# Seven of sixteen gate-weighted expert sums moved from VectorE to ScalarE and GpSimd

## The reference, cut to what matters

```
h      = swiglu(flat @ W1_shared)                  # 512 hidden numbers a row
routed = 0
for e in range(8):
    routed = routed + h @ W2_experts[e] * w[:, e:e + 1]   # w: the gate of row and expert
out = x + (shared + routed)
y   = rmsnorm(out) ; x = x + layernorm(y)
```

## Time and profile before

| what | value |
|---|---|
| median of three runs | 2315.79 us |
| the profiled execution, its own time | 2326.53 us |
| its span | 2324.5 us |
| TensorE busy | 2059.2 us (89%) |
| VectorE busy | 1385.1 us (60%) |
| ScalarE busy | 831.0 us (36%) |
| GpSimd busy | 342.1 us (15%) |
| mean clock granted to TensorE | 0.881 of full speed |

### The profile page before, as it was taken

One profiled execution on the slowest core, in us unless ns is written; L12 is line 12 of the kernel. 1 busy time (PEld: TensorE's weight loads), 2 busy tenths in 40 slices (PEclk: granted clock), 3 DMA queues, 4 the chain that ended last, 5 costly groups with the idle time before them and its releaser, 6 DMA issues.

```text
span 2324.5 us, 31756 instructions
## 1 busy us (share of the span) xinstructions
PE 2059.2 (89%) x9200; PEld 1081.4 (47%) x9200; DVE 1385.1 (60%) x4293; ACT 831.0 (36%) x1714; POOL 342.1 (15%) x647
## 2 busy tenths in 40 slices
PE   6868799898999989999898988989889999999986
PEld 4343445535364443635445353453635445354445
DVE  6456455755757465674667556476575745747454
ACT  2423424262433424334242532326233252423410
POOL 3322113101320003100031011210112001210000
PEclk7566889998998987989899898799899897889998
DMA  4003002010030101201021000211002110020212
GB/s 165 2 28 136 1 2 92 37 38 10 9 130 1 48 1 66 72 2 48 1 83 56 31 17 1 83 55 38 11 2 100 37 48 1 7 90 34 74 55 91
DMA packets 23089, 104.69 MB, mean 45 GB/s; under 512 B 3312, under 2 KB 14192, under 8 KB 18288
## 3 DMA queue, kind: packets, MB, share of 16 engines
q1 hardware_dynamic: 21168, 89.81, 10.7%
q0 software_dynamic: 1728, 12.58, 1.4%
HBM read 84.56 MB, written 16.78 MB: 44 GB/s over the span
## 4 chain that ended last, share of the span: by engine, by line
PE 68%; DVE 20%; issue 7%; ACT 3%; DMA 1%; DVEq 0%; POOL 0%; SPq 0%; POOLq 0%; ACTq 0%
PE fb L734 13%; PE fb L712 11%; PE sm L646 10%; PE ot L686 10%; PE st L672 5%; PE st L615 3%; DVE negmax L1013 2%; DVE acc L1201 2%; DVE stats L927 2%; PE st L631 2%; PE dn L615 2%; PE dn L654 2%; PE dn L698 2%; PE sm L672 2%; DVE sm L1010 1%
## 5 line engine op out<-in xcount | busy, mean ns | idle before, releaser
L536 ACT ACTIVATE probs<-st 128x512 f32<-128x512 f32 (+3 forms) x832 | 404.7, 506 | 486.1 <-PE st L672 438.6
L646 PE MATMUL sm<-k_t,q_t 48*128 48x512 f32 (+3 forms) x928 | 385.8, 496 | 102.6 <-DVE negmax L1010 49.3
L734 PE MATMUL fb<-w_r,h_r 128*128 128x512 f32 x1536 | 444.9, 426 | 13.2 <-DVE acc L1201 13.2
L1013 DVE TENSOR_REDUCE negmax<-sm 128x1 f32<-128x512 f32 x464 | 302.1, 686 | 136.2 <-PE sm L646 135.5
L646 PEld LDWEIGHTS sm<-k_t,q_t 48*128 48x128 f32 x928 | 170.8, 213 | 439.4 <-DVE negmax L1010 211.3
L672 PE MATMUL st<-q_t,k_t 64*128 64x512 f32 (+3 forms) x832 | 352.2, 478 | 14.3 <-ACT probs L536 12.1
L734 PEld LDWEIGHTS fb<-w_r,h_r 128*128 128x128 f32 x1536 | 279.8, 195 | 126.4 <-issue 60.1
L712 PE MATMUL fb<-xn_t,wup_s 128*128 128x512 f32 x512 | 321.5, 723 | 6.5 <-DVE h_s L1186 4.1
L1010 DVE CUSTOM_DVE_ANT_0 sm<-sm,mask_qk 128x384 f32<-128x384 f32 (+2 forms) x464 | 213.3, 467 | 190.9 <-PE sm L646 188.5
L686 PE MATMUL ot<-probs,v_s 128*32 128x512 f32 (+3 forms) x2048 | 276.3, 563 | 2.9 <-POOL probs L439 1.8
L672 PEld LDWEIGHTS st<-q_t,k_t 64*128 64x128 f32 x832 | 153.2, 203 | 135.1 <-ACT probs L536 87.1
(11 more groups left out here) (166 smaller groups left out, 2464.1 us busy)
## 6 DMA issues: line engine op xcount, KB each, us to landing
w_r<-w_parts SPq DMA_DIRECT2D x32, 2048.0 KB, 7.8
w_parts<-w_r POOLq DMA_DIRECT2D x4, 2048.0 KB, 8.9
x_s<-in_L_attn_query SPq DMA_DIRECT2D x8, 512.0 KB, 4.6
h_s<-in_L_ffn_W_experts POOLq DMA_DIRECT2D x8, 512.0 KB, 6.3
q_t<-rot_b SPq DMA_DIRECT2D x256, 4.0 KB
x_kept<-o_s SPq DMA_DIRECT2D x8, 512.0 KB, 3.0
xa<-x_kept SPq DMA_DIRECT2D x8, 512.0 KB, 3.5
out<-acc SPq DMA_DIRECT2D x8, 512.0 KB, 11.4
```

Source lines behind the costliest of these rows:

```text
L536: nc.scalar.activation(probs[:, n % PSLOTS, 0:hi - lo], score_bank(m)[:, 0:hi - lo], ACT.Exp, scale=float(D) ** -0.5).then_inc(s_ex, 1)
L646: mm(max_bank(w)[:, 0:hi - lo], q_t[r:r + MROW, b, t * P:(t + 1) * P], k_t[r:r + MROW, b, lo:hi], start=True, stop=True).then_inc(s_sm, 1)
L734: last = mm(fb[q % 2][:, :], h_r[:, h, m, rows], w2_r[:, k % 2, w, m, :], start=(m == 0 and n == 0), stop=(m == NH - 1 and n == 2))
L1013: return v.tensor_reduce(negmax[:, g % 2, n // GH, c:c + 1], max_bank(g * UNITS + n)[:, 0:hi - lo], AX.X, ALU.max, negate=True).then_inc(s ...
```

## The change

Seven sets leave VectorE's list: 4, 5 and 6 (the middle) and 9 to 12 (the lead of attention 1). For these ScalarE multiplies both halves of the PSUM bank by their gates into `scaled[q % 2]`, which is a view of `sg`, and signals the bank as read; GpSimd adds the two halves to `acc`, one after the other. In the middle ScalarE does its three sets between the centring and the copy of the transposed rows; in the lead it does each one step behind the set's last matmuls. GpSimd does sets 4 to 6 ahead of the low parts of the second heads stage, and 9 to 12 behind them. VectorE waits for the adds (s_ad) before its own next set. A further small step tells ScalarE that the gates are ready. The last batch does the same seven sets the same way.

```
+SCALED_MID, SCALED_LEAD = (4, 5, 6), (9, 10, 11, 12)
+SCALED = SCALED_MID + SCALED_LEAD
+        scaled = [sg[:, p, :].rearrange("p (e n) -> p e n", e=2) for p in range(2)]
...
 (gpsimd)
+            def add_scaled(f, outs):
+                for q in outs:
+                    t, n = (q - NT) % NT, SCALED.index(q)
+                    pool.wait_ge(s_er, f * N_ER + q + 1)
+                    g.tensor_tensor(acc[:, t, :], acc[:, t, :], scaled[q % 2][:, 0, :], ALU.add).then_inc(s_ah, 1)
+                    pool.wait_ge(s_ah, f * N_AH + n + 1)
+                    g.tensor_tensor(acc[:, t, :], acc[:, t, :], scaled[q % 2][:, 1, :], ALU.add).then_inc(s_ad, 1)
...
                 mask_probs(i, i - 1)
+                add_scaled(i - 1, SCALED_MID)
                 low_parts(i, 1)
+                add_scaled(i - 1, SCALED_LEAD)
             for n in range(NH):
                 hidden_low(B - 1, n)
+            add_scaled(B - 1, SCALED)
...
 (scalar)
+                    if f is not None and a == 1:
+                        for q in SCALED_LEAD:
+                            if OUT_AT[NH * OUT_BESIDE.index(q) + NH - 1] + ACT_LAG == m:
+                                scale_out(f, q)
...
+            def scale_out(f, q):
+                k, t = divmod(q - NT, NT)
+                n = SCALED.index(q)
+                act.wait_ge(s_eo, f * N_EO + q + 1)
+                act.wait_ge(s_er, f * N_ER + q)
+                if n == 0:
+                    act.wait_ge(s_gate, f + 1)
+                same = [m for m in range(n) if SCALED[m] % 2 == q % 2]
+                if same:
+                    act.wait_ge(s_ad, f * N_AD + same[-1] + 1)
+                for half in range(2):
+                    last = nc.scalar.activation(scaled[q % 2][:, half, :], fb[q % 2][:, half * E:(half + 1) * E], ACT.Copy,
+                                                scale=gate[:, t, 2 * k + half:2 * k + half + 1])
+                last.then_inc(s_er, 1)
...
                 centre(i)
+                if f is not None:
+                    for q in SCALED_MID:
+                        scale_out(f, q)
                 copy_rows(i, 2)
...
 (vector)
-                signal(v.tensor_tensor(gate[:, :, 0:EPG], ew[:, :, :], gate[:, :, EPG:NE], ALU.subtract))
+                done(v.tensor_tensor(gate[:, :, 0:EPG], ew[:, :, :], gate[:, :, EPG:NE], ALU.subtract))
+                v.memset(spare[:, :], 0.0).then_inc(s_gate, 1)
...
             def expert_out(f, q):
+                if q in SCALED:
+                    return
...
                 dve.wait_ge(s_er, f * N_ER + q)
+                dve.wait_ge(s_ad, f * N_AD + sum(n < q for n in SCALED))
...
             def finish(f):
                 dve.wait_ge(s_er, (f + 1) * N_ER)
+                dve.wait_ge(s_ad, (f + 1) * N_AD)
```

More of the change, by code:

```diff
@@ L223, in build @@
         s_er, N_ER = sem("expert_out_read"), OUTS
+        s_ah, N_AH = sem("first_scaled_part_added"), len(SCALED)
+        s_ad, N_AD = sem("scaled_parts_added"), len(SCALED)
+        s_gate = sem("gates_ready")
         s_xk, s_xb = sem("x1_stored"), sem("x1_loaded_back")
@@ L544, in attention @@
                             gate_exp(f, GATE_EXPS_AT.index(m))
+                    if f is not None and a == 1:
+                        for q in SCALED_LEAD:
+                            if OUT_AT[NH * OUT_BESIDE.index(q) + NH - 1] + ACT_LAG == m:
+                                scale_out(f, q)
+                    if f is not None and a == 0:
                         for n in range(2 * NH):
@@ L599, in _ @@
             hidden_high(B - 1, 2 * NH - 1)
+            for q in SCALED:
+                scale_out(B - 1, q)
         @block.tensor
@@ L1195, in expert_out @@
                     return
-                if q == NT:
+                if q == min(q for q in range(NT, OUTS) if q not in SCALED):
                     settle()
```

## The result

The changed kernel took 2342.95 us (17 runs, 2324.67 to 2374.09) against 2313.97 for the kernel before on the same chips: a ratio of 1.0111, with a 95% interval of 1.0081 to 1.0142. It is slower; the forecast was 2294 and the range ended at 2320. Medians here are of all runs; the ratios compare fast runs alone, those within 1.5% of their kernel's fastest. What happened begins as rival C has it (one long wait before the transposes, a fall of the clock behind it), and most of the loss stands in the lead, where C had none.

A forecast was written before the change was run, and what follows sets the result against it. TensorE was taken as the bound, with most VectorE adds standing behind it. Lead -12.9, middle +3.5 and clock -12 gave -21.4 us on 2326.53, so 2305.1; less 10.7 for that execution lying above the median, 2294. Range 2268 to 2320.

The forecast's parts named there:

- rival C: Middle: idle time before the transposes passes 3 us, clock falls every time, +2.9 us a batch, 2336 us; chance 0.12.
- What bounds the kernel: Whole kernel: most VectorE adds stand behind TensorE, so taking 54 us of busy time from VectorE gains that much nowhere.
- The lead, 1.84 us a batch: Lead of attention 1: two TensorE waits of 0.97 us shrink to about 0.05, gaining 12.9 us in seven batches.
- The middle: Sets 4 to 6: the wait before set 6 goes, but GpSimd's adds block VectorE; +0.5 us a batch, +3.5 in all.
- one piece of 3 us: Middle: TensorE's idle time gathers into a single wait of 3 us before the transposes.
- for which I add 0.3: Middle: allowance of 0.3 us a batch for low clock, since three of seven 1.87 us waits were followed by it.
- full blocking: Middle: VectorE stands until each GpSimd add ends; upper bound +1.3 us a batch, up to +4.7 with low clock.
- The clock's -12: Lead and attention 1: low clock behind the lead's second wait costs 25 us; half is taken as gained.
- A: Both gains in full: adds slip past VectorE and the lead's low stretch goes; 2263 to 2276 us; chance 0.15.
- B: The clock gives nothing back: -12.9 + 3.5 = -9, so 2306 us; chance 0.28 together with D.
- D: The change doesn't do what it says: GpSimd not hidden, VectorE waiting for its adds; chance 0.28 together with B.
- Its own signs: Profile after: 2 to 3 us wait before transposes, 0.5 to 0.8 us tiny steps, transposes to first score 1.8 us shorter.

The follow-up runs named there:

- e1: Changed kernel with only the lead's sets 9 to 12 moved; sets 4 to 6 stay with VectorE: 2293.86 us, ratio 0.9912 to the kernel before.
- e2: Changed kernel with only the middle's sets 4 to 6 moved; sets 9 to 12 stay with VectorE: 2370.51 us, ratio 1.0222 to the kernel before.
- e7: Changed kernel with only sets 4 and 9 to 12 moved; sets 5 and 6 stay with VectorE: 2339.88 us, ratio 1.0121.
- e12: Changed kernel plus 3 thrown-away matmuls at the start of the lead, the 2.8 us wait before the transposes left: 2298.05 us, ratio 0.9962.
- e4: Changed kernel with GpSimd's adds of sets 4 to 6 held back until VectorE has centred the rows, a tile per scaled set: 2298.96 us, ratio 0.9944.
- e8: e1 plus six GpSimd adds in the middle whose result nobody uses, two behind each of sets 4 to 6: 2305.71 us, ratio 0.9968.
- e6: e4 plus 4 thrown-away matmuls behind set 6, in its 1.0 us wait before the transposes: 2318.88 us, ratio 1.0005.
- e9: Changed kernel plus 12 thrown-away matmuls in the wait before the transposes and 3 at the start of the lead: 2258.33 us, ratio 0.9765.
- e10: e6 plus 3 thrown-away matmuls at the start of the lead: 2279.41 us, ratio 0.9869 to the kernel before.

## Why the prediction was wrong, point by point

- *What bounds the kernel.* Right: little of VectorE's 54 us was on the path.
- *The lead, 1.84 us a batch.* Right as a mechanism: e1's waits are gone and nothing took their place in six of seven batches. In the changed kernel it bought nothing in the lead, which ran at the low clock (31.7 us, and 31.6 in e2 with the adds still there).
- *The middle.* The mechanism was right, and its sum half a us too long. ScalarE's scaling of a set takes 0.84 us (0.8 to 1.1 expected), GpSimd's two adds 1.55 (1.55). Set 5's adds cost the tiny steps 0.86 us in the batch shown (1.2), set 6's cost the centring 0.96 (1.0), set 4's nothing (0.2). The transposes came 20.93 us behind attention 0, where the sum had 21.45, and the wait before them is 2.8 us, "one piece of 3 us".
- *The step that failed:* "three of seven such waits of 1.87 us were followed by the low clock, for which I add 0.3". The wait had become longer and had moved to another place, and I priced it by how often the old one was followed by a fall. The clock fell around its end, from 0.5 us ahead to 1.7 us behind, in 7 of 7 batches; in e2, e7 and e12, with waits of 2.0 to 2.9 us there, it fell in all seven too. Its direct cost is 2.5 us a batch (26.8 us instead of 24.25 to the start of the lead), near C's 3.4.
- *The term that no case had.* The second fall, at the start of the lead: the lead took 31.7 us where e1 needs 23.2, so 8.5 us a batch. The wait of 0.88 us behind which it begins stood in the trace of the kernel before, and the prediction's list of waits in the lead leaves it out. C has the right sign, place and first cause. That its 2336 lies 7 us from the measured median is luck: it adds 1.3 us a batch for full blocking, where the middle became 0.3 shorter, counts the lead's gain of 1.84 in full, has no second fall, and nothing for the gain of 2.1 us a batch behind the first score; the errors cancel.
- *The clock's -12.* The gain behind the first score came, -14.8 us, the whole of the 15 that I had halved, and e2 shows that it comes from the lead's sets. The four long low stretches of the kernel before lasted 13.7 to 20.5 us, not 15 to 22. e1, which leaves the middle untouched, measured 2294, by chance the number forecast for the whole change.
- *The rivals.* A's condition (adds slip past VectorE) is excluded by the stretched steps; B (2306) by the result; D by the profile. C had 0.12, and the rows spoke for more: four batches at full speed behind two separate waits said nothing of one wait in another place.
- *Its own signs.* The wait of 2 to 3 us ended by the centring came (2.77), so did tiny steps of 0.59 us and a lead without its 0.97 us waits. The distance from the transposes to the first score became 7.3 us a batch longer instead of 1.8 shorter, and the lead kept a low clock, which the prediction names as a sign that it is wrong.

The blocking itself is shown by e4 (adds moved away: steps at 0.16, rows 1.8 us earlier) and by e8 (adds alone: steps stretched). It agrees with the Trainium skill ("SBUF — State Buffer", section Who interferes with whom) for the steps with two inputs (0.16 us became 0.59, up to the end of GpSimd's add). The 128x4 TENSOR_SCALAR steps of e8, which have one tile as input, were stretched as well, from 0.17 to 0.47 and 0.57 us.

Open: why the 0.88 us wait at the lead's start is followed by a fall in some kernels and not in others. The kernel before has that wait and never fell there; e6 has less idle time ahead of it than e4 and fell in as many batches, for longer. e1 fell there once with no more waiting ahead of it than the kernel before has. The runs show that filling the wait ends the falls (28 of 28 batches in one profile each of e9 to e12), not what makes it harmful. Matmuls of the same kind at another place of the lead weren't tried. Executions of one kernel also differ: e6 had two at 2285 and 2288 among ten above 2313.

## What to carry to other kernels

Where TensorE is the bound, removing a wait of its own is only half of an edit: ask where its idle time stands afterwards, in how long a piece, and what runs behind it, since a fall of the clock can cost more than the wait and can come again tens of microseconds later. A cheap probe is to fill the suspected wait with matmuls into a free bank: if the kernel gets faster, the wait was paid in clock, and the filler (15 matmuls a batch took the changed kernel from 1.1% above the kernel before to 2.3% below) is a fix too. A probe that finds nothing proves less: four matmuls in e4's 1.0 us wait gave no gain, because a wait further on still cost the clock, and with that one filled too e10 was 1.3% under the kernel before. Work moved to GpSimd cost VectorE time where it met steps with two inputs in SBUF, the centring and some 128x4 steps with one; put it beside steps that read PSUM, as the maxima of the lead, or where VectorE waits, as in e4.

## What the runs showed of the hardware that was not expected

- Two falls of TensorE's granted clock to 1.2 GHz per batch from one edit, the second 20 us after the first had ended, with no wait over 0.6 us between them but the last, of 0.88; once low, the lead stayed low for up to 27 us though TensorE was busy 4.00 of 4.00 us.
- Less idle time didn't always mean more clock: e6 against e4, ratios 1.0005 and 0.9944. Their intervals touch, so that e6 is slower is likely and not shown; that it isn't faster is plain.
- A kernel with a wait of 3.0 us ahead of a set of twelve matmuls (e8, 0.9968) lost less than one with 2.1 us ahead of the transposes (e7, 1.0121), though the two differ in other work as well.
- VectorE's centring, one tile and two columns as inputs, was held up by GpSimd's adds (2.34 us instead of 1.38), and the maxima from PSUM were not (0.692 and 0.691 us).
